# A two-layer hybrid block on one core: GpSimd raises the norms' variances to the power -1/2, the ternary maps' sigmoid becomes a hyperbolic tangent, and the second layer's four orders of work are new

## The reference, cut to what matters

```python
x = x + L1_attn_a(layernorm(x))   # tag r:  gates, values = split(x W + b); h = scan(sigmoid(gates), tanh(values))
x = x + L1_ffn(layernorm(x))      # tag t1: silu(x Wu) * (x Wg) @ Wd, the three weights ternary
x = x + L1_attn_b(layernorm(x))   # tag l (two norms), gates ga and gx, a scan, tag n2 (a second norm), a gelu MLP (tag m)
x = x + L1_ffn(layernorm(x))      # tag t2: the same ternary map again

def layernorm(x, eps=1e-5): return (x - mean(x)) / sqrt(var(x) + eps)
def rmsnorm(x, w):          return w * x / sqrt(mean(x * x) + 1e-8)
def ternary(w):             s = mean(abs(w)) + 1e-8; return clip(round(w / s), -1, 1) * s
```

## Time and profile before

| | |
|---|---|
| three executions | 1555.21, 1555.29, 1556.89 us |
| span of the profiled execution, first to last instruction | 1552.6 us |
| PE matmul busy | 1461.9 us, 94% |
| DVE busy | 1146.4 us, 74% |
| ACT busy | 1025.5 us, 66% |
| POOL (GpSimd) busy | 683.1 us, 44% |
| mean granted TensorE clock | 0.978 |
| the second layer | from about 1268 us to the end |

### The profile page before, as it was taken

One profiled execution on the slowest core, in us unless ns is written; L12 is line 12 of the kernel. 1 busy time (PEld: TensorE's weight loads), 2 busy tenths in 40 slices (PEclk: granted clock), 3 DMA queues, 4 the chain that ended last, 5 costly groups with the idle time before them and its releaser, 6 DMA issues.

```text
span 1552.6 us, 23668 instructions
## 1 busy us (share of the span) xinstructions
PE 1461.9 (94%) x8388; PEld 1216.8 (78%) x8388; DVE 1146.4 (74%) x2615; ACT 1025.5 (66%) x2254; POOL 683.1 (44%) x804
## 2 busy tenths in 40 slices
PE   6989999999999998998999999999999987978898
PEld 5778888888888886786888888888886865655676
DVE  6988898989898985756766756666766649787646
ACT  3898989888898986454665655655654445564654
POOL 5657666676666554143433333333320511712233
PEclk8999999999999999998999999999999998988999
DMA  2000000000000000601000000000005122000000
GB/s 85 11 1 1 18 1 18 1 18 18 1 8 1 8 1 2 257 1 49 21 22 7 28 21 8 28 22 15 1 8 216 44 108 83 1 0 1 1 0 28
DMA packets 14341, 45.12 MB, mean 29 GB/s; under 512 B 3216, under 2 KB 3216, under 8 KB 12048
## 3 DMA queue, kind: packets, MB, share of 16 engines
q1 hardware_dynamic: 14224, 43.61, 7.8%
HBM read 42.55 MB, written 1.05 MB: 28 GB/s over the span
## 4 chain that ended last, share of the span: by engine, by line
PE 66%; DVE 18%; ACT 12%; issue 2%; POOL 1%; DMA 0%; SPq 0%; DVEq 0%; ACTq 0%; POOLq 0%
PE ps L149 25%; PE ps L348 15%; PE ps L1172 8%; PE ps L337 8%; DVE a_pT_lo L404 3%; ACT a_pT_hi L396 3%; PE ps L1946 2%; PE ps L1952 2%; ACT a_o_two L651 2%; DVE a_prob L357 2%; ACT a_prob L364 2%; DVE a_q L682 1%; PE ps L1962 1%; DVE f_r L1562 1%; PE ps L1965 1%
## 5 line engine op out<-in xcount | busy, mean ns | idle before, releaser
L379 POOL TENSOR_SCALAR a_prob<-a_prob,a_rowinv 128x128 f32<-128x128 f32 (+7 forms) x256 | 188.8, 749 | 132.2 <-DVE a_rowinv L373 132.2
L364 ACT ACTIVATE a_prob<-a_prob,a_negmax 128x128 f32<-128x128 f32 (+7 forms) x256 | 198.2, 781 | 21.5 <-DVE a_negmax L357 20.4
L404 DVE TENSOR_TENSOR a_pT_lo<-ps,a_pT_hi 128x512 fp32r<-128x512 f32 (+3 forms) x384 | 193.6, 551 | 24.4 <-ACT a_pT_hi L396 21.4
L357 DVE CUSTOM_DVE_ANT_0 a_prob<-ps,a_mask 128x128 f32<-128x128 f32 (+7 forms) x256 | 188.0, 750 | 14.5 <-PE ps L149 14.4
L379 POOL TENSOR_SCALAR b_prob<-b_prob,b_rowinv 128x128 f32<-128x128 f32 (+7 forms) x128 | 94.2, 748 | 234.7 <-DVE b_rowinv L373 234.7
L396 ACT ACTIVATE a_pT_hi<-ps 128x512 fp32r<-128x512 f32 (+3 forms) x384 | 164.3, 493 | 26.1 <-PE ps L348 20.5
L337 PE MATMUL ps<-ident,a_prob 128*128 128x128 f32 x1152 | 158.1, 275 | 7.6 <-DVE a_pT_lo L404 5.3
L364 ACT ACTIVATE b_prob<-b_prob,b_negmax 128x128 f32<-128x128 f32 (+7 forms) x128 | 99.7, 779 | 82.5 <-DVE b_negmax L357 82.2
L337 PEld LDWEIGHTS ps<-ident,a_prob 128*128 128x128 f32 x1152 | 129.8, 140 | 27.7 <-issue 12.8
L149 PE MATMUL ps<-a_k_hi,a_q 128*128 128x512 f32 (+3 forms) x384 | 138.4, 368 | 5.4 <-DVE a_negmax L357 5.3
L348 PE MATMUL ps<-a_pT_hi,a_v 128*128 128x512 f32 (+3 forms) x384 | 132.7, 353 | 4.5 <-DVE a_v L714 2.4
(11 more groups left out here) (452 smaller groups left out, 4169.3 us busy)
## 6 DMA issues: line engine op xcount, KB each, us to landing
f_wq<-in_f_wq SPq DMA_DIRECT2D x2, 2048.0 KB, 8.4
f_wo<-in_f_wo SPq DMA_DIRECT2D x2, 2048.0 KB, 17.6
b_w_raw<-in_b_qk SPq DMA_DIRECT2D x16, 256.0 KB, 2.6
a_w_raw<-in_a_w SPq DMA_DIRECT2D x8, 384.0 KB, 3.3
a_o_raw<-in_a_o SPq DMA_DIRECT2D x8, 256.0 KB, 2.7
f_wk<-in_f_wk SPq DMA_DIRECT2D x2, 1024.0 KB, 10.2
f_wv<-in_f_wv SPq DMA_DIRECT2D x2, 1024.0 KB, 12.3
f_wg<-in_f_wg SPq DMA_DIRECT2D x2, 1024.0 KB, 19.6
```

The source lines that it names most:

```text
L357: dve.tensor_tensor_reduce(slot(a, u), g.ps_flat[:, bank * HALF:bank * HALF + width], a.mask[:, N - width:], -1.0, -MASKED, ALU.add, ALU.m ...
L364: act.activation(prob, prob, ACT.Exp, bias=a.negmax[:, n:n + 1], scale=-1.0, accum_out=a.rowsum[:, n:n + 1]).then_inc(*g.exped.mark(a.tag, u))
L379: pool.tensor_scalar(prob, prob, a.rowinv[:, n:n + 1], 1.0, ALU.mult, ALU.mult).then_inc(*g.normed.mark(a.tag, u))
L404: dve.tensor_tensor(lo, src, fr(hi), ALU.subtract).then_inc(*g.lo.mark(a.tag, u, j0 // 4))
```

## The change

Three things are changed, all in the second layer.

1. The square roots of the norms leave ScalarE. `half_variance_dve` adds eps on VectorE, `half_root_pool` raises the result to the power -0.5 on GpSimd, a tensor of 128x4 to the power of a constant tensor `l.power`; the reciprocal on VectorE goes with it. In l the second root goes the same way, with one more small addition on VectorE.
2. In the ternary maps ScalarE computes tanh(s u / 2) in place of sigmoid(s u), and VectorE (1 + tanh) u in place of s u sigmoid; the factor s / 2 goes into the next product, as `l.both` = (s_up / 2) s_gate.
3. The four order strings are new.

```diff
+def half_variance_dve(dve, q, tag, eps):
+    dve.wait_ge(*q.pe.at(tag, "var"))
+    dve.tensor_scalar(q.std[:], q.bank[1][:, 0:HT], eps, None, ALU.add).then_inc(*q.dve.mark(tag, "var"))
+    yield
+def half_root_pool(l, pool, q, tag):
+    pool.wait_ge(*q.dve.at(tag, "var"))
+    pool.tensor_tensor(q.inv[:], q.std[:], l.power[:], ALU.pow).then_inc(*q.pool.mark(tag, "rec"))
+    yield
-def half_root_act(g, act, q, tag, eps):
-    act.activation(q.std[:], q.bank[1][:, 0:HT], ACT.Sqrt, bias=g.eps[:, k0:k0 + 1]).then_inc(*q.act.mark(tag, "std"))
 def half_inverse_dve(g, dve, q, tag):
-    dve.wait_ge(*q.act.at(tag, "std"))
-    dve.reciprocal(q.inv[:], q.std[:]).then_inc(*q.dve.mark(tag, "rec"))
-    dve.wait_ge(*q.dve.at(tag, "rec"))
+    dve.wait_ge(*q.pool.at(tag, "rec"))
     diagonal(g, dve, q.diag[:], q.inv[:]).then_inc(*q.dve.mark(tag, "diag"))
...
-        act.activation(q.sg[:, f % 2], q.bank[0], ACT.Sigmoid, scale=l.scale[:, 0, 0:1]).then_inc(*q.act.mark(tag, "sg", f))
+        act.activation(q.sg[:, f % 2], q.bank[0], ACT.Tanh, scale=l.scale[:, 0, 1:2]).then_inc(*q.act.mark(tag, "sg", f))
...
-        dve.scalar_tensor_tensor(sg, q.bank[0], s_up, sg, ALU.mult, ALU.mult).then_inc(*q.dve.mark(tag, "silu", f))
+        dve.scalar_tensor_tensor(sg, sg, 1.0, q.bank[0], ALU.add, ALU.mult).then_inc(*q.dve.mark(tag, "silu", f))
...
-        dve.scalar_tensor_tensor(q.hid[:, f % RING], q.bank[1], s_gate, sg, ALU.mult, ALU.mult).then_inc(*q.dve.mark(tag, "made", f))
+        dve.scalar_tensor_tensor(q.hid[:, f % RING], q.bank[1], l.both[:], sg, ALU.mult, ALU.mult).then_inc(*q.dve.mark(tag, "made", f))
...
-L1_POOL = '0000100110112112022212121011211212122222211111212212222'
+L1_POOL = (
+    "0000100020012111112112211221122111221111112211212222111121112222222")
```

61 lines of the change are left out of this document (36 added, 25 removed).

## The result

The changed kernel takes 1569.26 us (median of 6 runs, 1568.35 to 1571.29) against 1555.25 for the kernel before in the same rounds (6 runs, 1547.38 to 1556.89): a ratio of 1.0108, 95% interval 1.0084 to 1.0132. It is slower by about 1%, and outside my range. The profiled execution took 1570.5 us, its span is 1569.3: a difference of 1.2 us, where my sum had added 2.7 to a span.

What follows compares the result with a forecast made beforehand. Bound by chains through PE, DVE and ACT in turn, with no engine full before 1480 us. Start +9.7 and gains -13.5 make -3.8: span 1548.8, plus 2.7 gives 1551.5 us; own range 1546 to 1557, whole range 1543 to 1562.

Steps and rivals of the forecast that it cites:

- ScalarE: Second layer: 18 table loads and 12 roots less, 26.3 us of ACT, of which only what PE waits for counts.
- The power: GpSimd's power in each norm: 0.6 us, bounds 0.32 and 1.31; link to the diagonal 1.1 us, old one 0.7 without load.
- l of the first half: PE's 1.38 us wait for the diagonal: two powers replace a load, two roots and a load behind them, -0.9 us.
- About five of the twelve powers stand bare: Powers of r, t1, two of l (first half) and n2 (second) lie on PE's path; at 1.31 us each, +3.5 us.
- The start, first product of r: Start of the layer: the power waits behind splits through ga, first product at 1293.9 us, about 11.3 us late.
- so I take 22: First product of r to the second half's last x: 22 us for 24.5 before, ternary comparisons filling DVE's wait; range 20 to 26.
- The gains behind the start: From t1 on: first beats, l, load, sum of squares, gelus and n2 together -13.5 us; t2 nothing.
- The load of 1383 us: Table load at 1383.07 us is on PE's path; tanh needs none behind exp and tanh: -1.3 us.
- The sum of squares: n2 at 1400.20 us: 3.93 us on DVE beside the split of down, 0.7 once that is done early: -3.5 us.
- Rival 2: Inverse root waits in POOL's queue: start costs 14 us, gains only 8, +6 us, 1561 us; chance 0.18.
- rival 3: The power is long: 1555 us at 1.31 us each, 1567 us at 3.76; chance 0.07.

Runs made afterwards that it cites:

- e8: Changed kernel with each of GpSimd's twelve powers done twice, the first into a spare tile: ratio 1.0208, layer 305.1 us.
- e17: e5 with both powers of l of the first half directly behind the second part of the split of up: ratio 1.0023.
- e5: Kernel before with the new arithmetic (powers on GpSimd, tanh) in the old orders, powers of r directly behind the split of r: ratio 1.0033.
- e10: e5 without the tanh: powers on GpSimd with the sigmoid kept, in the old orders: ratio 1.0043.
- e1: Changed kernel, only GpSimd's order differs: both powers of r directly behind the split of r, ahead of the other splits: 1569.17 us, ratio 1.0114.
- e4: Kernel before, only GpSimd's order differs: all nine splits first, ahead of the first ring row: ratio 1.0066.
- e13: Kernel before, unchanged, profiled a second time: layer 275.1 us, where the first profile had 280.7.
- e3: Changed kernel with both edits of GpSimd's order, powers of r directly behind the split of r and splits spread between ring rows: 1561.95 us, ratio 1.0046.
- e2: Changed kernel, only GpSimd's order differs: splits of gx, out, up and down spread between ring rows, powers of r left in place: ratio 1.0070.
- e11: e5 with all nine splits in one row directly behind the powers of r: ratio 1.0099.

## Why the prediction was wrong

It saw the loss at the start and put less than half of its size there, since it charged only the queue: it let VectorE's operations run at their old length beside the splits.

- **ScalarE: right in size.** 18 loads less, 24.9 us less busy against 26.3 forecast, each load 1.28 us with no drain to be seen.
- **The power: too short.** 1.01 us for 0.6, inside my bounds but for two of the twelve (1.44 and 1.47). The link is 1.33 us for the 1.1 of my sum, and the old link without a load was 0.55 for 0.7. So a link that had no load was to cost 0.4 us more and costs 0.8; with a load of its own on the path it was to gain 0.9 and gains 0.7. At l of the first half, where I had taken off 0.9 us, PE's wait is 1.34 for 1.38. "About five of the twelve powers stand bare" was too few for the 10.0 us of e8. By e17, e5 and e10 the powers, in the places that I gave them, cost 0.2 to 0.4% of the kernel, 4 to 7 us, where my sum had a gain from ACT's relief.
- **The start, first product of r: right.** I forecast it 11.3 us late by the queue, it was 12.5. But it did not set the end of the stretch: e1 took 5 us of it away and the first `up` moved by 0.9.
- **The start, "so I take 22": the step that failed.** From the first product to the last x of the second half it took 33.5 us (1297.43 to 1330.29 + 0.69), against a range of 20 to 26. I counted on DVE using its wait for ternary comparisons. It did, but a ternary product took up to 4.38 us for 1.28. The row was in front of me: I had read the sum of squares of 3.93 us beside the split of down as a gain to come, and did not ask which operations of DVE the nine early splits would stand beside. That is the term that was mis-sized, 33.5 us for 22: 11.5 of the 14.1 us by which the first `up` missed its forecast (24.8 us late, not 10.7). The sum itself had slipped too, by half a microsecond: its terms from 1316 us on add up to 1323.05, not 1322.5.
- **The gains behind the start: smaller, and of another origin.** From first `up` to the end I forecast 13.5 us less. Against the first profile of the kernel before it is 10.5 us less, against the second (235.6 us) 5.3. e4, which has none of the arithmetic, has 8.1 of the 10.5. So most of them come from the splits being gone from t1 and n2, not from ScalarE; against the second profile e4 has 2.9 of 5.3.
- **The load of 1383 us: half right.** PE's wait stayed at 3.10 us where I had taken off 1.3, since DVE was next late; the root behind it did come sooner.
- **The sum of squares: 3.5 us were one outcome of two,** as e13 shows, where it took 1.96 us and PE waited 0.68.
- **Rival 2** named the right sign, though 1561 us is still 8 us short (1567 us, the far end of rival 3, is nearer, by a power of 3.76 us that it did not take). Its signs were met: the first `up` came after 1326 us, and the gains behind it were under 9.7 us against one of the two profiles. Even so its mechanism, the queue, is not what held the changed kernel's start, by e1; it counts once the splits are spread (e3 against e2). Rival 3 has a share: the power's length counts. The first power took 1.03 us, about as the others, and started as soon as the split ahead of it ended: the 6 us of a first call that the Trainium skill gives (GPSIMD Engine Reference, Instruction dispatch) do not show here, and no row says if this was such a call.

What stays open: what the powers would cost in better places of the queues, and how the 0.09% between e11 and the changed kernel (3.7 us of layer in single profiles) divides among the new orders, if it is there at all.

## What to carry to other kernels

When work is moved on GpSimd, list what VectorE does beside its new place: here operations with both operands in SBUF were held until GpSimd's ended, so was a comparison of one tensor in SBUF, and the scaled values that read PSUM were not. In this kernel a split is best placed beside the latter, and what stands behind it on GpSimd has to be looked at too: moving the split of down from one link only held another. And a wait that is taken from a queue is worth nothing until the next thing that is late has been named: here the start of r ended with the last split, whenever it began.

A chain that passes through engine after engine feels what its links grow by: 12.3 us more of power made this layer 10.0 us longer. Relief counts by place and not by sum: 16 loads and the 12 roots less on ScalarE lost to longer and queued links, while three loads less, one of them ahead of a root that the scans wait for, gained. The small edit inside the large one is worth trying alone. And a term taken from one row needs a second profile of the same code first.

## What was not expected of the hardware

- GpSimd's power of 128x4 numbers takes 1.01 us, three times the 0.32 us of a sum of 128x64 in this kernel.
- A hold works both ways: that power took 1.99 us beside a two-operand product of VectorE that had begun 0.16 us before it (e5).
- The same code had a layer of 275.1 and of 280.7 us; 2 us of that are one sum of squares that met the 1.9 us half of a split or the 3.8 us half. The changed kernel, with no split in that place, repeats to 0.2 us and its 6 runs lie within 3 us, where 6 of the kernel before lie within 9.5.
